# A graph kernel on one core: the running maximum turned back in transpose mode, and a window of 32 nodes

## The reference

```python
# layer 0
agg_sum = segment_sum(x[src], dst);  deg = segment_sum(1, dst)
hp = relu(x @ W_pool + b_pool)
agg_max = segment_max(hp[src], dst)
out1 = batch_norm(x @ W_self1 + (agg_sum / max(deg, 1)) @ W_neigh1, g1, beta1)
out2 = batch_norm(x @ W_self2 + agg_max @ W_neigh2, g2, beta2)
x = layernorm(x + leaky_relu(out1 + out2))
# layer 1, 8 heads of 12
K, Q, V = x @ Wk + bk, x @ Wq + bq, x @ Wv + bv;  E = edge_attr @ We + be
score = exp(clip(sum_in_head(K[src] * Q[dst] / sqrt(12) * E), -5, 5))
h = segment_sum(V[src] * score, dst) / (segment_sum(score, dst) + 1e-6)
x = layernorm(x + h)
```

## Time and profile before

| | |
|---|---|
| median of 3 runs | 4438.12 us (4435.52 to 4441.56) |
| profiled execution | 4438.06 us, span 4436.3 us |
| mean granted TensorE clock | 0.989 |
| PE busy | 4362.1 us (98%) |
| PEld busy | 3921.0 us (88%) |
| POOL busy | 3123.4 us (70%) |
| DVE busy | 2229.0 us (50%) |
| ACT busy | 1420.3 us (32%) |
| chain of waits, by engine | PE 96%, DVE 1%, issue 1%, POOL 1% |
| line 1019, matmuls | 832.0 us, 3232 records |
| gathers, line 394 | 1538.0 us (layer 0) and 1557.6 us (layer 1), 1613 records each |

### The profile page before, as it was taken

How to read it: one execution, slowest core, us unless ns; L and a number is a source line. 1 busy time by engine, 2 the same in 40 slices (tenths; PEclk the granted TensorE clock), 3 DMA queues, 4 the chain that set the end, 5 groups by cost and what they waited for, 6 DMA issues and landing times.

```text
span 4436.3 us, 109751 instructions
## 1 busy us (share of the span) xinstructions
PE 4362.1 (98%) x32762; PEld 3921.0 (88%) x32762; DVE 2229.0 (50%) x5236; ACT 1420.3 (32%) x3823; POOL 3123.4 (70%) x3252
## 2 busy tenths in 40 slices
PE   8999999999999999999989999999999999999996
PEld 7989899999999898989858999999999999999996
DVE  5444444444444444444455555555555555555556
ACT  3333333333333333333243333333333333333333
POOL 7776776777766767667517777777777777777774
PEclk9999999999999999999989999999999999999997
DMA  3111111111111111111124444444444444444442
GB/s 88 38 36 36 36 36 36 36 37 36 37 36 36 37 36 36 36 36 37 27 63 119 116 116 116 116 117 114 117 116 116 116 117 115 116 117 117 116 116 78
DMA packets 209077, 333.35 MB, mean 75 GB/s; under 512 B 73181, under 2 KB 156824, under 8 KB 208952
## 3 DMA queue, kind: packets, MB, share of 16 engines
q0 software_dynamic: 129040, 238.05, 22.6%
q1 hardware_dynamic: 80008, 94.94, 6.9%
HBM read 325.49 MB, written 7.24 MB: 75 GB/s over the span
## 4 chain that ended last, share of the span: by engine, by line
PE 96%; DVE 1%; issue 1%; POOL 1%; ACT 0%; DMA 0%; SPq 0%; POOLq 0%; ACTq 0%; DVEq 0%
PE bank L1019 17%; PE bank L1143 9%; PE bank L1121 9%; PE bank L1129 9%; PE bank L1138 8%; PE bank L988 8%; PE bank L999 8%; PE bank L1160 8%; PE bank L1010 6%; PE bank L1028 6%; PE bank L990 4%; PE bank L1152 1%; POOL kvg L394 1%; PE bank L1069 1%; PE bank L1070 1%
## 5 line engine op out<-in xcount | busy, mean ns | idle before, releaser
L394 POOL DMA_INDIRECT kvg<-in_x_dram,idx x1613 | 1538.0, 954 | 648.4 <-issue 638.7
L394 POOL DMA_INDIRECT kvg<-kv_table,idx x1613 | 1557.6, 966 | 509.0 <-issue 459.9
L1019 PE MATMUL bank<-ident,scan 96*128 96x96 f32 x3232 | 832.0, 400 | 0.0
L667 DVE TENSOR_TENSOR acc<-acc,bank 97x64 f32 (+1 forms) x808 | 177.5, 220 | 1244.7 <-PE bank L1010 949.9
L1019 PEld LDWEIGHTS bank<-ident,scan 96*128 96x128 f32 x3232 | 787.3, 328 | 0.0
L551 ACT COPY eaC<-bank 96x512 f32<-96x512 f32 x404 | 234.7, 581 | 1119.2 <-PE bank L1121 1108.7
L473 ACT COPY scanE<-bank 128x384 f32<-128x384 f32 x404 | 193.1, 478 | 1225.5 <-PE bank L1019 1225.5
L1028 PEld LDWEIGHTS bank<-S,scanE 128*96 128x96 f32 x3232 | 339.6, 165 | 216.0 <-issue 214.0
L657 DVE TENSOR_TENSOR_SCAN scan<-keepC,scan,bank 96x512 f32<-96x512 bf16 x404 | 513.1, 1270 | 0.0
L642 DVE TENSOR_TENSOR S<-iotaW,rel 128x512 f32<-128x512 f32 (+1 forms) x808 | 445.8, 552 | 25.5 <-issue 25.5
L1143 PE MATMUL bank<-qwin,scan 64*128 64x96 f32 x3232 | 456.0, 281 | 0.0
(11 more groups left out here) (125 smaller groups left out, 5038.4 us busy)
## 6 DMA issues: line engine op xcount, KB each, us to landing
ea<-in_edge_attr_dram SPq DMA_DIRECT2D x402, 192.0 KB, 2.5
kvg<-in_x_dram,idx POOLq DMA_INDIRECT x1613, 2.5
kvg<-kv_table,idx POOLq DMA_INDIRECT x1613
kv_table<-stage SPq DMA_DIRECT2D x6, 672.0 KB, 3.3
stage<-counts_row SPq DMA_DIRECT2D x1, 2352.0 KB, 12.9
xN<-in_x_dram SPq DMA_DIRECT2D x6, 336.0 KB, 3.3
out_dram<-xN SPq DMA_DIRECT2D x6, 336.0 KB
src_all<-in_src_groups_dram SPq DMA_DIRECT2D x1, 804.0 KB
```

What stands on the lines that cost most here:

```text
L394: pool.indirect_dma_start(out=to[:, r, j, :], out_offset=None, in_=table, in_offset=bass.IndirectOffsetOnAxis(ap=idx[:, r, j:j + 1], axis= ...
L1019: last = pe.matmul(bank[4 + b][:, j * D:(j + 1) * D], scan[:, b, j:GE:J], ident[0:D, 0:D], start=True, stop=True)
```

## The change

Line 1019 uses `pe.transpose`, as line 1098 does, with the same operands in the same order. W becomes 32, and with it the free size of S, the window's columns in `acc`, and the window tiles `xwin`, `qwin` and `stC`. A small early temporary (`baseB`) that lives in S spans two of its four parts. Every engine's instructions stand in the same order as before; only sizes, and the mode of line 1019, differ.

```diff
@@ -26,7 +26,7 @@
 R = 4
 TURNS = -(-(FULL + 1) // R)
 NG = TURNS * R
-W = 64
+W = 32
@@ -83,7 +83,7 @@
         S = sb("S", [P, R, 2 * J, W])
-        baseB = S[:, 0, :, :].rearrange("p j w -> p (j w)")[:, 0:NG]
+        baseB = S[:, 0:2, :, :].rearrange("p r j w -> p (r j w)")[:, 0:NG]
@@ -1016,8 +1016,7 @@
                     pe.wait_ge(s_scan, ready(i, r))
                     pe.wait_ge(s_bcp, freed(i, r, 2))
                     for j in range(J):
-                        last = pe.matmul(bank[4 + b][:, j * D:(j + 1) * D], scan[:, b, j:GE:J], ident[0:D, 0:D],
-                                         start=True, stop=True)
+                        last = pe.transpose(bank[4 + b][:, j * D:(j + 1) * D], scan[:, b, j:GE:J], ident[0:D, 0:D])
                     last.then_inc(s_back, 1)
```

## The result

The changed kernel takes 4374.83 us (median of 4 runs, 4366.96 to 4381.64) against 4439.34 before: a ratio of 0.9855, 95% interval 0.9837 to 0.9873. It is faster, by 64 us (1.5%) where 168 were forecast; 4375 lies above the range of 4245 to 4325.

What follows compares the result with a forecast made beforehand. The prediction took PE to bound the kernel, busy 98%, with POOL close behind in both layers. Its terms, 130 + 14 + 3 + 21 = 168 us, took 4438 to 4270 us; range 4245 to 4325.

Steps and rivals of the forecast that it cites:

- Layer 0's terms (130 + 14 + 3): Layer 0: 130 us from running at POOL's pace, 14 from PE's backlog at the end, 3 from the last three iterations.
- POOL's 5.061: POOL's own period in layer 0, us a group: gathers end to end 4.993, plus 0.068 for its own stalls.
- Line 1019's record: Layer 0, transpose mode: 4 records of 0.236 us a group, saving PE 0.95 us; bounds 1.53 and no saving.
- W of 32 in layer 1: Layer 1: 32 fewer columns save 0.027 us at each of lines 1129 and 1160, 21 us; bounds 0 and 35.
- The clock: Rival 3: pauses drop layer 0's clock, costing nothing up to half-clock share f = 0.24; hard form 4635 us, chance 0.04.
- the rival's mild form: The mild clock: layer 0 at half clock for a share f near 0.3, 5.25 us a group, 4352 us; chance 0.06.
- Rival 1: Layer 1 doesn't gain: tile switch costs the same at 32, or POOL has no pace below 5.08; 4291 us, chance 0.20.
- Rival 2: Line 1019's strided load keeps all its cost, layer 0 stays at 5.41 us a group; 4417 us, chance 0.05.
- rival 4: POOL is no floor in layer 0: gathers speed up, PE's saving comes through whole; 4033 us, chance 0.02.

Runs made afterwards that it cites:

- window_only: The kernel before with only W = 32, line 1019 still a matmul: 4920.9 us, ratio 1.109.
- transpose_only: The kernel before with only line 1019 in transpose mode, W still 64: 4327.81 us, ratio 0.9761.
- pe64_dve32: The changed kernel with PE's tiles 64 wide again, while DVE and ACT keep windows of 32: 4286.12 us, ratio 0.9652.
- all_but_agg_narrow: pe64_dve32 with PE's tiles in layer 1 narrow at lines 1128, 1142 and 1151, while line 1159 moves 64 columns: 4285 us.
- narrow_k64_split: pe64_split with PE's tiles in layer 1 narrow at lines 1128, 1151 and 1159, 64 rows at line 1142: 4256.4 us, ratio 0.9602.
- pe64_split: pe64_dve32 with layer 0's one-hot made by two DVE instructions of 128 elements: 4265.13 us, ratio 0.9609.
- onehot_split_w64: transpose_only with layer 0's one-hot made by two DVE instructions of 256 elements, not one of 512: 4300.5 us, ratio 0.9691.

## Why the prediction was wrong

**Layer 0's terms (130 + 14 + 3): right in sum, 147 against 150.** POOL sets the pace once PE is fast enough, PE's further gain is lost to waiting, and PE's backlog at the end goes. Forecast and measured: last gather near 2058 and 2052.5 us; last block of "ends" near 2071 and 2067.5; 5.061 and 5.057 us a group from start to start. One by one the three terms are 136, 11 and 3 us.

**Inside them, two errors cancel.** POOL's 5.061 was 4.993 plus 0.068 for stalls with gaps of 2.07 us, which I took for POOL's own. None of those is left: idle time is 434.3 us for 1425 gathers, 0.305 each, and no kernel whose PE is ahead in layer 0 has one. window_only, where POOL waits behind PE still longer, has 256 gaps over 1.2 us. So they came with the wait behind PE. In their place the gathers are longer, 959 ns on average against 944 for an undisturbed one, 0.06 us a group, by the DVE blocks. With W = 64 they take 985 ns (transpose_only), and the forecast of layer 0 would have been 40 us off. That it came out at W = 32 is luck: the shorter one-hot did it, a part that I had costed at nothing, since DVE is busy 50%.

**Line 1019's record: 0.13 us and not 0.236.** I took the nearest row; the truth lay nearer the other bound of 0.09. PE's own group is 4.00 us and not 4.46. It moved nothing, since POOL sets the pace at either.

**The step that failed is "W of 32 in layer 1", a gain of 21 us; measured, that loop lost 85.** It counted the narrow tiles only as shorter blocks at full clock and put their effect on the clock at nothing, since PE never pauses there. The clock fell to half all the same, in 20 bursts of dips between the first and the last gather. With the 11 us that the loop gains at full clock (below) they cost 85 + 11 = 96 us, nearly 5 in each. Where PE's tiles are 64 wide and all else is kept (pe64_dve32), no burst is left and the loop is back at 5.08.

**Its 21 us at full clock were half right.** A group takes 5.05 us there and not 5.08 (forecast 5.03). The blocks from line 1129 on before, and the same blocks after:

```profile
3005.96 1.09 PE L1129 MATMUL bank<-ident,S 128*64 128x128 f32 x8
3006.89 0.33 PE L1152 MATMUL bank<-w_q,xwin 97*64 97x96 f32 x2
3007.15 0.94 PE L1160 MATMUL bank<-S,msg 128*104 128x64 f32 x8
3007.93 1.08 PE L1138 MATMUL bank<-w_e,eaC 97*128 97x96 f32 x8
3008.94 1.13 PE L1143 MATMUL bank<-qwin,scan 64*128 64x96 f32 x8
```

```profile
2240.71 1.06 PE L1128 MATMUL bank<-ident,S 128*32 128x128 f32 x8
2241.61 0.33 PE L1151 MATMUL bank<-w_q,xwin 97*32 97x96 f32 x2
2241.87 0.92 PE L1159 MATMUL bank<-S,msg 128*104 128x32 f32 x8
2242.62 1.11 PE L1137 MATMUL bank<-w_e,eaC 97*128 97x96 f32 x8
2243.66 1.13 PE L1142 MATMUL bank<-qwin,scan 32*128 32x96 f32 x8
```

Both forecast savings of 0.027 us came: the block of S went from 0.93 to 0.90, with its first interval at the forecast 0.13, and line 1160's from 0.78 to 0.75. But the next block, line 1138, went from 1.01 to 1.04 and gave the second one back. In all_but_agg_narrow, where line 1159 stays wide, neither changes and the group is 5.05 again. So 0.027 a group, 11 us, was to be had. narrow_k64_split is 8.7 us under pe64_split by the medians, a difference inside the intervals.

**The clock was a rival in the wrong place.** I had it fall in layer 0, where PE would come to pause, and took a PE that never pauses as safe, on the strength of one dip that ended so. In layer 0 it was at half for a share f of 0.10, less than in the rival's mild form (0.3) and below the f of 0.24 from which it costs, and cost nothing, as the rival's own sum says. In layer 1, with PE busy throughout, it fell too.

The rule of the Trainium skill ("TensorE: Matmul & The Clock Gate", Part 4, PE-mode transpose) that I weighed, that transpose-mode work doesn't count as a busy PE, is neither borne out nor excluded. From 60 to 2000 us, layer 0 of transpose_only dips 12 times, and 7 to 18 times in the three other runs with the same layer 0, where the kernel before has no dip. With the same transposes and tiles on PE and shorter one-hots on DVE it dips 0 to 3 times (0 in pe64_dve32), and window_only, with line 1019 a matmul, has most of all, 192. What brings the few dips at W of 64 is open.

By its number the mild clock (4352) came nearest to 4375, with the clock in the other loop. Rival 1 (layer 1 doesn't gain, 4291) is excluded too: its two reasons don't hold, as layer 1 has a faster pace at full clock. Rival 2 is excluded by 1616 records, 0.51 us a group, and rival 4 by the 5.05 us of POOL.

## What to carry to other kernels

Time on the busiest engine is a bound only until the next one's bare pace: read that pace from a stretch in which it doesn't wait, before counting on a saving. Making tiles smaller can be a loss even where no instruction gets longer at full clock. In this kernel the granted clock went with which of the tiles were narrow, and padding them on TensorE alone gave back 89 us. So look at the clock in the stretches of the loop, not in the page's digits, and try the padding. And an engine at 50% can still hold up another by the length of its single instructions; splitting one long instruction in two cost DVE time and gained 27 us (onehot_split_w64).

## What the runs showed of the hardware that I had not expected

- The clock fell to 0.82 in a loop in which PE was busy throughout (window_only, layer 0), when 16 of its records a group moved 32 columns and not 64 in the same time.
- In transpose mode a record whose weights are loaded with a step of 4 elements takes 0.13 us (line 1019), against 0.09 with adjacent ones (line 1098). As a matmul the same strided load makes it 0.236, against 0.11 for adjacent ones (line 988, 96 columns too).
- Changing the size of the tile once more in a group of matmuls (line 1128 at 32 columns, line 1151 at 64) took 0.1 us more a group at full clock, 5.18 against 5.08.
- A long gather that starts during a DVE one-hot ends 0.82 us after it, whatever the length of the one-hot (0.69 us in transpose_only, 0.43 in the changed kernel), and one that starts in the first of two isn't held up by the second.
- In layer 1 a narrower line 1159 gained 0.03 us a group, and the block after it, with its tiles unchanged, took 0.03 us longer.
